# Who does the second layer normalisation of an attention block: GpSimd behind the inverse deviation, or VectorE in the next half step

## What is computed

```python
def _layernorm(x, axis=-1, eps=1e-05):
    m = jnp.mean(x, axis=axis, keepdims=True)
    v = jnp.var(x, axis=axis, keepdims=True)
    return (x - m) / jnp.sqrt(v + eps)
...
x = _layernorm(x + _L0_attn_ref(x, L0_attn_wq, L0_attn_wk, L0_attn_wv), axis=-1)
x = _layernorm(x + _L0_xattn_ref(x, ctx_1024, ctx_1024, mask_Bx1x1xS2_ik0, ...), axis=-1)
x = _layernorm(x + _L0_ffn_ref(x, L0_ffn_router_w, ...), axis=-1)
```

## Time and profile before

| | |
|---|---|
| median of 3 runs | 2143.32 us (2142.54 to 2143.4) |
| profiled execution | 2142.94 us, of which the span from first to last instruction is 2140.8 |
| TensorE matmuls | 2042.3 us, 95% of the span |
| VectorE | 1301.8 us, 61% |
| ScalarE | 989.1 us, 46% |
| GpSimd | 840.1 us, 39% |
| mean granted TensorE clock | 0.98 |
| attention stage | up to about 1547 us |

### The profile page before, as it was taken

The page is one execution under the profiler, slowest core; times in us unless marked ns, Lnnn a source line. Parts: engine busy times, 40 slices in busy tenths (PEclk is TensorE's granted clock), DMA queues, the critical chain, the costliest instruction groups (busy, mean ns, idle before and its releaser), DMA issues. The chain is left out here.

```text
span 2140.8 us, 55059 instructions
## 1 busy us (share of the span) xinstructions
PE 2042.3 (95%) x21891; PEld 1516.0 (71%) x21891; DVE 1301.8 (61%) x2740; ACT 989.1 (46%) x1515; POOL 840.1 (39%) x1134
## 2 busy tenths in 40 slices
PE   7899999999999999999999999988699999999996
PEld 4667777777776777777777767766478787878785
DVE  5678778788778787787887787865211111111146
ACT  1455555555555555555555555544231212121233
POOL 3333454544444444545445444432412121212144
PEclk8899999999999999999999999998899999999998
DMA  3331112111011111000111100100123323332363
GB/s 97 98 114 51 43 40 82 36 58 43 28 39 30 30 34 38 29 28 26 31 35 28 32 26 25 31 21 19 53 50 87 72 33 84 87 72 33 84 228 148
DMA packets 99531, 118.80 MB, mean 55 GB/s; under 512 B 12144, under 2 KB 92221, under 8 KB 97232
## 3 DMA queue, kind: packets, MB, share of 16 engines
q1 hardware_dynamic: 69856, 83.75, 12.4%
q0 software_dynamic: 17184, 19.66, 5.2%
q10 hardware_dynamic: 12240, 11.88, 1.6%
HBM read 66.11 MB, written 56.12 MB: 57 GB/s over the span
## 5 line engine op out<-in xcount | busy, mean ns | idle before, releaser
L992 DVE TENSOR_REDUCE smax<-ps_s 128x4 f32<-128x1024 f32 x508 | 619.2, 1219 | 209.4 <-PE ps_s L661 197.4
L868 ACT ACTIVATE prob<-ps_e 128x1024 f32<-128x1024 f32 x508 | 519.7, 1023 | 466.5 <-PE ps_e L674 327.0
L1833 ACT ACTIVATE hid<-m_ps_h,b_sb 128x320 f32<-128x320 f32 x256 | 134.7, 527 | 392.4 <-PE m_ps_h L1787 392.4
L661 PE MATMUL ps_s<-stack_kh,stack_q 32*128 32x256 f32 x2032 | 305.3, 307 | 0.8 <-ACT stack_q L857 0.8
L674 PE MATMUL ps_e<-stack_q,stack_kh 32*128 32x256 f32 x2032 | 293.7, 281 | 0.0
L1787 PE MATMUL m_ps_h<-m_cols,w_sb 128*128 128x320 f32 x1024 | 292.4, 435 | 0.6 <-DVE m_cols L1856 0.6
L674 PE MATMUL ps_e<-stack_q,stack_kl 32*128 32x256 f32 x2032 | 289.9, 277 | 0.0
L1804 PE MATMUL m_ps_o<-w_sb,hid 128*128 128x256 f32 x1280 | 279.2, 380 | 1.4 <-DVE m_res L1885 1.4
L661 PE MATMUL ps_s<-stack_kl,stack_q 32*128 32x256 f32 x2032 | 276.6, 278 | 0.0
L1804 PEld LDWEIGHTS m_ps_o<-w_sb,hid 128*128 128x128 f32 x1280 | 243.7, 190 | 35.9 <-DVE m_res L1885 1.8
L1676 POOL DMA_INDIRECT sums_dram<-m_res,m_token x70 | 108.2, 1546 | 399.7 <-DVE m_res L1920 346.5
(11 more groups left out here) (169 smaller groups left out, 3665.0 us busy)
## 6 DMA issues: line engine op xcount, KB each, us to landing
w_sb<-in_w SPq DMA_DIRECT2D x16, 1024.0 KB, 7.5
slot_rows_dram<-w_sb ACTq DMA_DIRECT2D x40, 258.0 KB, 2.8
m_rows<-slot_rows_dram SPq DMA_DIRECT2D x15, 645.0 KB, 4.8
xT<-in_xT SPq DMA_DIRECT2D x32, 256.0 KB, 3.0
ctxT<-in_ctxT SPq DMA_DIRECT2D x32, 256.0 KB, 2.8
x_res<-in_x SPq DMA_DIRECT2D x32, 256.0 KB, 2.8
sums_dram<-x SPq DMA_DIRECT2D x32, 256.0 KB
c_rows<-sums_dram SPq DMA_DIRECT2D x8, 1024.0 KB, 15.5
```

What stands on the lines that cost most here:

```text
L661: return nc.tensor.matmul(out, stack_q[at_side][rows, g, t * P:(t + 1) * P], (stack_kh, stack_kl)[part][at_side][rows, g, :], start=(X == ...
L868: nc.scalar.activation(prob[:, h:h + 2, :].rearrange("p h s -> p (h s)"), shifted[:, :, :, :].rearrange("p h t s -> p (h t s)"), ACT.Exp, ...
L992: nc.vector.tensor_reduce(max_columns(X, p), scores[:, :, :, :], AX.X, ALU.max)\
L1833: nc.scalar.activation(hid[:, m, half * HALF:(half + 1) * HALF], ps_h[:, (2 * m + half) % 4, 0:HALF], ACT.Gelu, bias=b1_sb[:, pe_, m:m + 1 ...
```

## The change

`second_normed` moves from VectorE's program to GpSimd's. There it stands directly behind `inverse_deviation` of the same cross item, in the half step before the one in which VectorE did it, and ahead of `residual_with_bias` and `place`. It waits for the same readers of the previous `x2` as before. The arithmetic is the same: two operations of 128x256, each subtracting a per-partition mean and multiplying by a per-partition `rstd`. VectorE's next instruction behind the maxima of tile 0 is now the maxima of tile 1.

```diff
@@ VectorE
-            def second_normed(b):
-                if x2_sent.due(b - 1):
-                    dve.wait_ge(x2_sent.sem, x2_sent.count(b - 1))
-                if x2T_mm.due(b - 1):
-                    dve.wait_ge(x2T_mm.sem, x2T_mm.count(b - 1))
-                if rows_sent.due(b - 1):
-                    dve.wait_ge(rows_sent.sem, rows_sent.count(b - 1))
-                normalise(CROSS, b, y2, x2)
...
-                    if is_of(CROSS, q) and k == 1:
-                        second_normed(q[1])
@@ GpSimd
+            def second_normed(b):
+
+                if x2_sent.due(b - 1):
+                    pool.wait_ge(x2_sent.sem, x2_sent.count(b - 1))
+                if x2T_mm.due(b - 1):
+                    pool.wait_ge(x2T_mm.sem, x2T_mm.count(b - 1))
+                if rows_sent.due(b - 1):
+                    pool.wait_ge(rows_sent.sem, rows_sent.count(b - 1))
+                pool.wait_ge(ln_r[CROSS].sem, ln_r[CROSS].count(b))
+                ready()
+                for t in range(T2):
+                    nc.gpsimd.tensor_scalar(x2[:, t, :], y2[:, t, :], mv[CROSS][:, t, 0:1], rstd[CROSS][:, t:t + 1],
+                                            ALU.subtract, ALU.mult).then_inc(ln[CROSS].sem, 1)
...
                 if is_of(CROSS, p):
                     inverse_deviation(CROSS, p[1])
+                    second_normed(p[1])
```

## The result

| | before | after |
|---|---|---|
| median of 4 runs each | 2142.93 us (2142.07 to 2143.4) | 2197.99 us (2193.93 to 2207.03) |
| profiled execution (span) | 2142.94 (2140.8) | 2197.59 (2195.6) |
| TensorE's mean granted clock | 0.980 | 0.969 |

The ratio is 1.0263 (95% interval 1.0231 to 1.0295): the kernel became 55 us, 2.6%, slower. The forecast was 2156.2 us in a range of 2144 to 2181. The sign and the chain of waits came as forecast, the size did not: the time lies 17 us above the range, and a cost appeared that the forecast did not have.

The account below looks back on a forecast made before the run. The prediction took TensorE's wait at tile 4, reached from GpSimd's `y` through VectorE, as the bound. 23 x 0.45 + 4 x 0.15 = 10.95 us, plus 1.98 at the attentions' end, gave 2156.2 us; range 2144 to 2181.

Parts of the forecast that it names:

- What bounds the kernel: Attention pairs: any delay of GpSimd's `y` passes through VectorE's statistics and tile 3's maxima to TensorE's tile 4 and the period.
- Part one: VectorE at tile 1: removing about 1.29 us of work per pair gains nothing, hidden behind waits for TensorE and ScalarE's `max_high`.
- Part two: GpSimd between `rstd` and `x1b`: two added operations at 0.90 us each plus a semaphore lengthen the queue by 1.98 us.
- rival 2: GpSimd's second arithmetic step is not free: 1.35 us per operation gives 2181.4 us, 1.80 gives 2206.7; chance 0.18.
- The semaphore: GpSimd's wait on `rstd` before the new operations: 0.18 us, as for `rstd` behind its own `veps`.
- The sum: Queue growth 1.98 us less 1.53 usable idle makes `y` 0.45 us late; 12.9 us in all, including the attentions' end.
- TensorE runs without a stop behind tile 4: TensorE in the attention pairs: a delay of tile 4 goes into the period, taken as the same 0.45 us.
- "Slower": Whole kernel: the chance of a time above 2147.6 us, set at 0.78.

Follow-up runs that it names:

- `x1b` behind `y`: Changed kernel with GpSimd's `residual_with_bias` (1.27 us) moved from in front of `y` to behind it in the self half steps: 2147.33 us, ratio 1.0008.
- statistics late: VectorE's statistics of `y` moved behind tile 3's maxima, `x1` behind tile 4's: 2128.87 us in the changed kernel, 2129.47 us in the kernel before.
- the gap (filled): Changed kernel with six unread 128x512 bf16 matmuls on TensorE in front of tile 4 of the self half steps: 2172.41 us, ratio 1.0129.
- The relief alone: Kernel before with VectorE's two operations on `x2` cut from 256 to 8 columns, GpSimd as before: 2143.25 us, ratio 1.000.

## Why the prediction was wrong, step by step

- **What bounds the kernel: right.** The chain `y`, statistics, maxima of tile 3, tile 4, period held link for link, and a run bears on each: the queue (`x1b` behind `y`), the order on VectorE (statistics late), the gap (filled).
- **Part one: right.** The relief alone gives 1.000. `max_low` stands 779.94 - 777.67 = 2.27 us behind tile 1, 2.29 before, with VectorE idle in front of it.
- **Part two, the price of one operation: too small.** 1219 ns, a third above the 0.90 us. The scaling from the one-step row was right (930 ns); the second arithmetic step, 289 ns, was the error. I had that as rival 2, with a chance of 0.18 and nothing against it but the nearest row. That row has one step, so the estimate for two should have stood above it. The GPSIMD Engine Reference of the Trainium skill (3.1, Elementwise) puts one and two arithmetic operations at the same rate, an estimate of 0.22 us here; both measured values disagree, with each other and with that.
- **The semaphore: 0.34 for 0.18 us.** I took the row of another pair of operations on the same engine.
- **The sum: right in form.** 0.34 + 2.42 = 2.76 us of queue, less the 1.58 us idle and 0.07 that the small routing operations give back, makes `y` 1.11 us late. The prediction's own sum with these values is 23 x 1.11 + 4 x 0.81 + 2.76 = 31.5 us, so 2174.8; the kernel with the filled gap measured 2172.4. The end of the attentions added 2.77 us for 1.98: from the last `rstd` to the first send behind it it is now 1578.27 - 1574.58 = 3.69 us, before 1522.03 - 1521.11 = 0.92.
- **"TensorE runs without a stop behind tile 4": the step that failed.** I let the period grow by as much as tile 4 comes late, and by no more. But idle time on TensorE had a second price here: behind gaps of about 1.6 us the granted clock fell to 0.50 in 15 of 26 pairs, which made each of them 1.5 to 2.0 us longer, 25.6 us together. The pairs of the kernel before could not show it, since their gaps were 0.5 us; its trace has half clock only at both ends of the attentions, at the start of the experts and at the end of the program. The end of the attentions held the one hint: from 1434 to 1478 us there are gaps of 0.83 to 1.58 us before score tiles, and three stretches at 0.50 between 1442.8 and 1483.8. Whether the one brought the other there, no run shows. The prediction should have had a rival in which a longer gap takes the clock along. The page TensorE: Matmul & The Clock Gate of the Trainium skill (A second HAM failure mode: psum-queue depth-cycling) tells of a kernel whose clock swings because TensorE idles briefly between groups of matmuls; the trace after agrees, with 15 falls behind gaps of about 1.6 us, and with none from 160 to 1425 us where the gap is filled.
- **Chances.** "Slower" had 0.78. The range ended at 2181, below the upper half of rival 2 (2206.7) and without the clock.

Open: why the clock fell in 15 pairs and not in the 11 others. The length of the gap does not part them: it is 1.58 to 1.95 us in the 15 and 1.29 to 1.61 in the 11, with 1.58 in both.

## What to carry to other kernels

An idle engine is a fit place for an operation only up to the slack of its queue in front of the next operation that others wait for; read that slack from one timeline (1.58 us here) and compare it with the whole insertion, the semaphore included. Where the queue's next result reaches the bound engine through another engine's order, look there first: moving the statistics behind the maxima gave 0.7% and made the whole question idle. And a gap on TensorE that grows past what the kernel had before can cost more than its length: at 0.96 us it did not, at about 1.6 us it did in 15 of 26 pairs. So its price has to be bounded with the half clock behind it.

## What the runs showed of the hardware

- GpSimd's tensor-scalar with per-partition factors, 128x256 in float32: 930 ns with one arithmetic step, 1219 with two; 128x512 with one step, 1563. The second step is not free.
- From `rstd` to `x2`, which waits for it on the same engine, GpSimd is idle for 0.34 us, from `veps` to `rstd` for 0.18.
- TensorE's granted clock stayed at 1.00 behind gaps of 0.49 and 0.96 us once per pair, and fell to 0.50 for 3.4 us behind gaps of about 1.6 us in 15 of 26 pairs. With matmuls of no use in the gap it stayed at 1.00. A pair with such a fall took 1.69 us more than one without.
